# Order of the work ahead of the loop in a three-stage tower kernel: tile 1's tables in buffers of their own, tile 0's b table on GpSimd

## The reference, cut to what matters

```python
# stage 1: 16 channels x 128 heads, 64 complex terms, 1024 positions
Wc = Wc * num * _reciprocal(den * Lam, EPS)
P = dt_Lambda[..., None] * pos - P_max[..., None]
h = jnp.einsum('chn,hnl->chl', Wc, jnp.exp(P)).real
# stage 2: a 1024x1024 weight, masked by blocks of 32x32
h = h + jnp.einsum('bsk,nk->bsn', _layernorm(h), w_masked)
# stage 3: base product, a router of 8 experts with sparsemax, and rank-16 experts
z = _layernorm(h)
h = h + (einsum(z, W_base) + b_base) + sum over experts of weights * (z @ lora_A) @ lora_B
```

## Time and profile before

| | |
|---|---|
| median of 3 runs | 555.26 us (554.86 to 555.58) |
| the profiled execution, time | 552.86 us |
| its span in the trace | 551.0 us |
| its mean granted TensorE clock | 0.978 |

### The profile page before, as it was taken

The page is one execution under the profiler, slowest core; times in us unless marked ns, Lnnn a source line. Parts: engine busy times, 40 slices in busy tenths (PEclk is TensorE's granted clock), DMA queues, the critical chain, the costliest instruction groups (busy, mean ns, idle before and its releaser), DMA issues.

```text
span 551.0 us, 7574 instructions
## 1 busy us (share of the span) xinstructions
PE 498.4 (90%) x2595; PEld 422.0 (77%) x2595; DVE 400.3 (73%) x854; ACT 268.6 (49%) x484; POOL 120.8 (22%) x109
## 2 busy tenths in 40 slices
PE   1446689988999999999999999999999999999995
PEld 0335578766888888888888888888888888888884
DVE  4989987898777777777777869687777677763341
ACT  1655447843918273645546363728191827232200
POOL 0463664713030303020110203030303030303030
PEclk9986879999999999999999999999999999999999
DMA  7991002001010101000010101010101010101011
GB/s 280 399 284 21 0 1 82 7 0 44 1 44 1 43 0 29 14 15 27 7 36 0 43 0 43 0 43 0 43 0 43 2 38 1 38 1 29 11 35 43
DMA packets 17244, 24.06 MB, mean 44 GB/s; under 512 B 9480, under 2 KB 11720, under 8 KB 17224
## 3 DMA queue, kind: packets, MB, share of 16 engines
q1 hardware_dynamic: 16704, 23.54, 14.2%
q10 hardware_dynamic: 520, 0.27, 0.2%
HBM read 15.41 MB, written 8.39 MB: 43 GB/s over the span
## 4 chain that ended last, share of the span: by engine, by line
PE 80%; DVE 13%; issue 2%; ACT 2%; DMA 1%; POOL 0%; ACTq 0%; DVEq 0%; POOLq 0%
PE acc_b L409 34%; PE acc_a L409 28%; PE turnp L386 5%; PE small L433 4%; PE turnp L395 2%; PE turnp L402 2%; PE small L435 1%; DVE mask_sum L970 1%; DVE wa_raw L979 1%; PE acc_b L369 1%; DMA lam_sb<-in_L_tok_Lambda 1%; DVE u_t L1009 1%; DVE wa_lo L986 1%; DVE tmp L1066 1%; DVE gh_t L1008 1%
## 5 line engine op out<-in xcount | busy, mean ns | idle before, releaser
L881 POOL TENSOR_TENSOR h<-h,st 128x1024 f32<-128x1024 f32 x16 | 30.5, 1905 | 349.9 <-PE turnp L402 334.6
L409 PE MATMUL acc_a<-wa_hi,x_hi 128*128 128x512 f32 x256 | 83.7, 403 | 1.9 <-DVE x_lo L1076 1.9
L409 PE MATMUL acc_b<-wb_hi,x_hi 128*128 128x512 f32 x256 | 85.2, 409 | 0.0
L409 PE MATMUL acc_a<-wa_lo,x_hi 128*128 128x512 f32 x256 | 81.0, 392 | 0.0
L409 PE MATMUL acc_a<-wa_hi,x_lo 128*128 128x512 f32 x256 | 80.8, 392 | 0.0
L409 PE MATMUL acc_b<-wb_lo,x_hi 128*128 128x512 f32 x256 | 80.6, 391 | 0.0
L409 PE MATMUL acc_b<-wb_hi,x_lo 128*128 128x512 f32 x256 | 80.5, 391 | 0.0
L617 ACT ACT_TABLE_LOAD x14 | 18.0, 1283 | 101.9 <-DVE b_sb L1068 101.7
L409 PEld LDWEIGHTS acc_a<-wa_hi,x_lo 128*128 128x128 f32 x256 | 48.5, 189 | 10.4
L409 PEld LDWEIGHTS acc_a<-wa_lo,x_hi 128*128 128x128 f32 x256 | 48.5, 190 | 10.1
L409 PEld LDWEIGHTS acc_b<-wb_lo,x_hi 128*128 128x128 f32 x256 | 48.1, 188 | 10.5
(11 more groups left out here) (179 smaller groups left out, 930.9 us busy)
## 6 DMA issues: line engine op xcount, KB each, us to landing
out<-h SPq DMA_DIRECT2D x15, 512.0 KB
mask_raw<-in_L_attn_mask SPq DMA_DIRECT2D x8, 512.0 KB, 10.6
wa_raw<-in_L_attn_weight SPq DMA_DIRECT2D x8, 512.0 KB, 11.2
wb_raw<-in_L_ffn_W_base SPq DMA_DIRECT2D x8, 512.0 KB, 14.8
xn<-in_x SPq DMA_DIRECT2D x15, 64.0 KB
wr_raw<-in_L_ffn_lora_A SPq DMA_DIRECT2D x8, 64.0 KB, 3.3
lb_raw<-in_L_ffn_lora_B SPq DMA_DIRECT2D x1, 512.0 KB, 3.7
bias<-in_L_ffn_b_base SPq DMA_DIRECT2D x1, 512.0 KB, 4.6
```

Source lines behind the costliest of these rows:

```text
L409: return pe.matmul(cols, a, rows, start=first, stop=last)
L881: pool.tensor_tensor(h2[par][:, :], h2[par][:, :], st2[:, par, 1:2].to_broadcast([P, L]), ALU.subtract)\
```

## The change

Seven edits, all ahead of the loop but for three.

1. Tile 1's tables have buffers of their own (`u_1`, `er_1`, `xy_1` and so on, laid over `h2[0]` and over `x1_raw`, the memory of `x1_lo`). `q_arguments(1)` and `phases(1)` stand right behind those of tile 0 on DVE, and `sines(1)` and `q_sines(1)` right behind those of tile 0 on ACT. `exponentials` no longer waits for a b table; `sines` does, from tile 2 on.
2. `table_v` is split: `v_factors` (up to `u12`) is called on its own, earlier, ahead of the loop. For tiles 0 and 1 the second product goes to PSUM (`turnp`), so that the sum reads one operand from PSUM.
3. The b table of tile 0 is made on POOL, right behind `parameters(0)`; `decay_b(0)` is called ahead of it on DVE. Tile 1's stays on DVE, tile 2's on POOL.
4. `BY_POOL` and `CENTRE_LAST` change: POOL makes the low halves of three row blocks (1, 3, 5) in place of four, and centres four (4 to 7) in place of six.
5. `k_low` reads the transposed product in PSUM in place of the copy in `b_sb`; `k_rows` therefore waits for `kt_lo`. This holds in the loop too.
6. In `reciprocal_deviation` the instruction with two tensor operands of one column becomes one with a tensor and two scalar columns. This holds in the loop too, as does the changed wait of edit 1.
7. The constants are issued second on SP's queue in place of first on ACT's; `mask_sums(0)` stands ahead of `signs()`, `dt_transposes()` ahead of `block_sums(0)`; the calls on PE, ACT, POOL and DVE are put in another order up to the loop, among them `phases(2)`, `phases(3)` and `table_v(2)`.

The diff, cut to its core; first buffers, waits and POOL's order, then table_v, k_low, the reciprocal, and the orders of DVE and PE:

```diff
-        BY_POOL = (1, 3, 4, 6)
-        CENTRE_LAST = 2
+        BY_POOL = (1, 3, 5)
+        CENTRE_LAST = 4
...
+        spare, spare_lo = h2[0], x1_raw
+        u_1, er_1 = h_n(spare[:, 0:HT * NM], NM), h_n(spare[:, HT * NM:2 * HT * NM], NM)
...
             sp.dma_start(ldt[:, :], log_dt).then_inc(ldt_in, 16)
+            sp.dma_start(kst[:, :], consts).then_inc(consts_in, 16)
...
             def k_rows(t):
                 pe.wait_ge(kt_hi, t + 1)
+                pe.wait_ge(kt_lo, t + 1)
...
             def exponentials(t):
                 act.wait_ge(tab_exponent, t + 1)
-                if later(t, 1):
-                    act.wait_ge(b_ready, t)
...
             def sines(t):
                 act.wait_ge(tab_phase, t + 1)
+                if later(t, 2):
+                    act.wait_ge(b_ready, 1 if at(t, 2) else t)
...
             def table_b(t):
                 pool.wait_ge(b_chain, t * 3 + 1)
-                pool.wait_ge(h1_ready, t)
-                pool.wait_ge(kt_lo, t)
+                if t > 0:
+                    pool.wait_ge(h1_ready, t)
+                    pool.wait_ge(kt_lo, t)
+                pool.wait_ge(v_chain, t * 4 + 3)
...
             parameters(0)
-            wa_centre(2)
-            wa_centre(3)
+            table_b(0)
+            wa_lows(1)
             wa_centre(4)
-            wa_lows(1)
+            wa_centre(5)
             wa_lows(3)
-            wa_centre(5)
-            wa_lows(4)
             wa_centre(6)
             wa_centre(7)
-            wa_lows(6)
+            wa_lows(5)
             parameters(1)
...
+                second = kt_heads if not later(t, 2) else tmp[:, :].rearrange("p (h a c) -> p h a c", h=HT, a=NA)
...
+                if at(t, 1):
+                    dve.wait_ge(h1_copied, t)
                 dve.wait_ge(v_chain, t * 4 + 3)
                 dve.tensor_tensor(whole(v_sb), w(0), u(0), ALU.mult)
-                dve.tensor_tensor(tmp4, w(1), u(1), ALU.mult).then_inc(v_chain, 1)
+                dve.tensor_tensor(second, w(1), u(1), ALU.mult).then_inc(v_chain, 1)
                 dve.wait_ge(v_chain, t * 4 + 4)
-                dve.tensor_tensor(whole(v_sb), whole(v_sb), tmp4, ALU.add).then_inc(v_ready, 1)
+                dve.tensor_tensor(whole(v_sb), second, whole(v_sb), ALU.add).then_inc(v_ready, 1)
...
-                dve.tensor_tensor(lo[:, :, :], kt_full, hi[:, :, :].bitcast(F), ALU.subtract).then_inc(kt_lo, 1)
+                by_head = lambda v: v[:, :, :].rearrange("p a (h c) -> p h a c", c=C)
+                dve.tensor_tensor(by_head(lo), kt_heads, by_head(hi).bitcast(F), ALU.subtract).then_inc(kt_lo, 1)
...
-                dve.scalar_tensor_tensor(s[:, 6:7], s[:, 5:6], s[:, 5:6], s[:, 4:5], ALU.mult, ALU.mult).then_inc(s_chain, 1)
+                dve.tensor_scalar(s[:, 6:7], s[:, 4:5], s[:, 5:6], s[:, 5:6], ALU.mult, ALU.mult).then_inc(s_chain, 1)
...
             phases(0)
             reciprocal_of_tanh(0)
+            q_arguments(1)
+            phases(1)
+            wa_mask(1)
             mask_sums(2)
-            wa_mask(1)
             mask_sums(3)
             wa_lows(0)
             wa_mask(2)
+            reciprocal_of_norm(0)
+            decay_b(0)
             mask_sums(4)
+            v_factors(0)
             wa_mask(3)
-            reciprocal_of_norm(0)
+            table_v(0)
+            wa_lows(2)
             mask_sums(5)
             wa_mask(4)
-            wa_lows(2)
-            table_v(0)
-            table_b(0)
             mask_sums(6)
-            q_arguments(1)
             wa_mask(5)
-            phases(1)
             mask_sums(7)
             wa_mask(6)
             k_low(0)
             wa_mask(7)
-            wa_lows(5)
+            wa_lows(4)
+            v_factors(1)
             table_v(1)
             table_b(1)
+            wa_lows(6)
             wa_lows(7)
...
             wa_transposes(6)
-            first_attention(0, range(3, 6))
+            first_attention(0, range(2, 4))
             wa_transposes(7)
-            first_attention(0, range(6, KC))
+            first_attention(0, range(4, 6))
...
+            x_transposes(2)
             wb_half(0)
+            wb_half(1)
+            first_attention(0, range(6, KC))
             pe.wait_ge(h1_copied, 1)
             k_transposed(1)
```

More of the change, by code:

```diff
@@ L240, in whole, with phases_of, er_of, sines_of @@
             return b[:, :, :, :]
[L242 to L244 removed]
+        def phases_of(t):
+            return (u_1, k_1, g_1, h_1, a_1) if at(t, 1) else (u_t[:, :, :], k_t, g_t, h_t, a_t[:, :, :])
+        def er_of(t):
+            return er_1 if at(t, 1) else er_t[:, :, :]
+        def sines_of(t):
+            return (xy_1, pp_1, qq_1) if at(t, 1) else (whole(xy), whole(pp), whole(qq))
+        def b_factors(t, i):
+            _, p_, q_ = sines_of(t)
+            return (p_[:, i].unsqueeze(3).to_broadcast([P, HT, NB1, NB0]),
+                    q_[:, i].unsqueeze(2).to_broadcast([P, HT, NB1, NB0]))
         def b_terms(b):
@@ L748, in _ @@
             act.activation(wr[:, :, 0, :], cat_raw, ACT.Copy).then_inc(cat_hi, 1)
-            wb_highs(10)
-            wb_highs(11)
+            wb_highs(4)
+            exponentials(2)
+            wb_highs(5)
+            wb_highs(6)
+            sines(2)
+            wb_highs(7)
+            wb_highs(8)
+            h2_centre(0, 0)
+            wb_highs(9)
+            k_copy(1)
+            for i in range(10, 13):
+                wb_highs(i)
+            h2_high(0)
             k_deviation(1)
-            h2_high(0)
-            wb_highs(12)
             wb_highs(13)
+            wb_highs(14)
             h2_deviation(0, 0)
-            wb_highs(14)
             wb_highs(15)
@@ L1018, in table_v, with v_factors @@
+            def v_factors(t):
                 heads = bass.ds(t * HT, HT)
+                xy_ = sines_of(t)[0]
                 def q(v):
                     return v[:, heads].unsqueeze(1).unsqueeze(3).to_broadcast([P, 2, HT, NA])
+                dve.wait_ge(tab_sin, t + 1)
+                dve.wait_ge(tab_exp, t + 1)
+                if not later(t, 3):
+                    dve.wait_ge(q_ready, 1 if t < 2 else 2)
+                dve.tensor_tensor(xy_, xy_, decay(t, SA, NA), ALU.mult).then_inc(v_chain, 1)
+                dve.wait_ge(v_chain, t * 4 + 1)
+                dve.tensor_tensor(whole(t1), xy_, q(qr), ALU.mult)
+                dve.tensor_tensor(whole(t2), xy_, q(qi), ALU.mult).then_inc(v_chain, 1)
+                dve.wait_ge(v_chain, t * 4 + 2)
+                dve.tensor_tensor(u12[:, 0], t1[:, 0], t2[:, 1], ALU.add)
+                dve.tensor_tensor(u12[:, 1], t1[:, 1], t2[:, 0], ALU.subtract).then_inc(v_chain, 1)
@@ L1023, in w, with table_v @@
+            def table_v(t):
                 def w(r):
@@ L1210, in _ @@
                             small[:, HALF - rt_rows:HALF].rearrange("p (e k) -> p k e", e=E)).then_inc(rt_copied, 1)
+            wb_lows(0)
+            wb_lows(1)
+            h1_reciprocal(0)
+            phases(2)
+            for i in range(2, 5):
+                wb_lows(i)
             k_low(1)
@@ L1219, in _ @@
             wb_lows(9)
-            table_v(2)
-            wb_lows(10)
-            wb_lows(11)
-            decay_b(2)
-            h2_low(0)
-            for i in range(12, 2 * NWT):
-                wb_lows(i)
-            phases(3)
+            decay_b(2)
+            v_factors(2)
+            phases(3)
+            for i in range(10, 13):
+                wb_lows(i)
+            h2_low(0)
+            wb_lows(13)
+            wb_lows(14)
+            wb_lows(15)
+            table_v(2)
             h2_reciprocal(0, 0)
```

178 lines of the change are left out of this document (82 added, 96 removed).

## The result

The changed kernel takes 546.49 us (median of 4 runs, 545.68 to 546.81), the kernel before 555.31 us beside it (554.86 to 555.58): 8.8 us less, ratio 0.984 with a 95% interval of 0.9823 to 0.9857. The profiled execution took 546.28 us, with a span of 544.5 us.

The account below looks back on a forecast made before the run. Prediction: DVE bounds the kernel up to 71 us, PE nearly after. Cumulative gains reach -8.4 us entering the loop; +1.2 for PE's clock gives -7.2, so 555.26 - 7.2 = 548.0 us, range 545.0 to 551.2.

Parts of the forecast that it names:

- The start: Up to `dec`: mask sum and transposes fall into DVE's hole before lambda lands, `dec` at 9.02 instead of 11.44, -2.4 us.
- Tile 0's product: Ahead of the loop on PE: starts at 35.5 instead of 43.0, -7.5 us, with its b table made on POOL.
- First attention product: PE starts attention at 49.0 instead of 55.3, -6.3 us, with `k_low` ending at 44.9.
- The hole: PE's long wait before tile 1's product moves but stays 6.6 us; restart 59.3 instead of 71.2, released by low halves.
- Router and gates: Router product at about 97.8 instead of 103.4, -5.6 us; PE's gates wait shrinks from 2.59 to about 0.4, -7.8 us.
- Edits costed at nothing: `k_low` from PSUM saves nothing, PSUM second product nearest 0, one-column form passes its stall on, counted as empty.
- rival A: DVE/POOL shared port takes it back: stalls return at 17 to 29 us; gain only 4.7, 550.6 us; chance 0.17.
- In the loop: Step stays 29.0 us; `k_rows` waiting for `k_low` has 2.1 us of cover and costs nothing.
- Rival C: Slower: `k_rows` waits for `kt_lo` every step; at 3.1 us late +6.8, 562 us; chance 0.04.
- The clock: PE at half clock behind its hole or at `k_rows`: 2.4 us more or nothing; half taken, +1.2 us.
- the offset of 2.4: Median of runs stands 2.4 us above the profiled execution, so 545.7 profiled became 548.0 us forecast.
- The range: Change in time from -9.5 to about -4 us, from bounds on POOL's b table, PSUM write, clock and start.

Follow-up runs that it names:

- Experiment 8: Changed kernel with the constants issued first on ACT's queue again, ahead of lambda's transfers; 547.75 us.
- Experiment 2: Changed kernel with tile 0's b table back on DVE behind its v table, off POOL; 550.35 us.
- Experiment 10: Changed kernel with the low halves of block 6 on DVE ahead of tile 1's b table, two calls exchanged; 543.53 us.
- Experiment 3: Changed kernel with phases(3) back at its old place behind table_v(2), POOL's b table of tile 2 not waiting for it; 549.55 us.
- experiment 6: Changed kernel with k_low reading the copy in SBUF again and k_rows not waiting for it, all 16 tiles; 548.67 us.
- experiment 5: Changed kernel with the second product of tile 0's v table in SBUF again, tile 1's staying in PSUM; 547.39 us.
- 7: Changed kernel with the one-column instruction in its old form with two tensor operands, in the loop too; 547.50 us.
- Experiment 1: Kernel before with only the change at the start (constants on SP's queue, first activation on ldt, mask sums and transposes earlier); 550.09 us.
- experiment 4: Changed kernel with the second product of tile 1's v table in SBUF, without the wait for h1; 546.17 us.
- 9: Changed kernel with tile 1's arguments and angles moved late into DVE's wait at 39.16, ACT's part behind wa_copies(4); 547.59 us.
- 11: Changed kernel with the last instruction of reciprocal_deviation also given a scalar pointer, so both one-column products have one; 543.75 us.
- 12: Changed kernel with four edits: block 6's low halves earlier, phases(2) in DVE's wait, tile 1's second product in SBUF, both scalar pointers; 539.96 us.

## Why the prediction was right, point by point

The forecast of 548.0 us was 1.5 us above the measured 546.49, inside its range. The chain it follows is the one in the trace, but three terms were mis-sized, and they partly cancel.

- **The start, forecast -2.4, measured -4.3 in the profile.** This term was mis-sized. I let DVE's signs begin where they had, behind lambda's landing at 8.3, and kept the earlier landing for the bounds, by no more than the 0.6 us of its issue. Ahead of the constants on its queue lambda has landed by 3.7. Experiment 8 puts it back: `dec` at 9.29, +1.3 us.
- **Tile 0's product, forecast 35.5, measured 33.46.** Of these 2.0 us 1.9 are the start's; the rest of that sum held: `u12` to product 6.3 us forecast, POOL's table 6.2 measured. Experiment 2 prices the table's place, forecast 3.5, at 3.9 by the medians and 2.3 in its profile, where 2.0 of new stall and 2.4 of a wait that shrank stand against each other.
- **First attention product at 49.0: right by luck, two errors cancelling.** `k_low` ended at 43.8, not at 44.9. But I left out the eight transposes of block 5 ahead of `k_rows`, 1.7 us at half clock, which wait for DVE's low halves (the row at 45.68 above). DVE's wait for block sums was 2.96, forecast "some 2". So of the 1.9 us that the start gave more, nothing was left here.
- **The hole**: forecast 6.6 us, restart 59.3, released by low halves; measured 6.39, 59.35. Experiment 10 shows that two calls in DVE's order make 2.8 us of it, which I had seen and taken as given.
- **Router and gates**: forecast 97.8 and a wait of 0.4; measured 98.0 and 0.19. Experiment 3 prices the move of `phases(3)` at 3.1 us, but not as my sum has it, by PE's wait: without the move PE comes to the gates earlier and waits longer, and it is the clock behind the wait that costs.
- **Edits costed at nothing.** For the change as a whole that was right, since I had charged no stall there. But it hid what they do, counted from `dec` to tile 3's product: `k_low` from PSUM is worth 1.5 us (experiment 6), tile 0's sum from PSUM 1.4 (5), the one-column form 1.2 (7). Each keeps a stall away that a wide instruction of POOL beside it would bring, in experiment 5 the b table, which is new there, in 6 and 7 work that POOL had before; "its operands were free already" looked at waits and not at the port. This is rival A's mechanism, and these edits are a part of why it did not come; all three undone together were not run.
- **In the loop**: step 29.0 in every profile, with and without `k_rows` waiting (experiment 6). Rival C is out.
- **The clock, forecast +1.2, and the offset of 2.4.** The cost was real but elsewhere: in the profile after, the granted clock falls at tile 3's product, as the stretch from 130 to 135 shows. In the profile before it did not fall there. The second and third row go from tile 3's product to the loop, after and before:

```profile
130.00:135.00 5.00, 4.94 (x29) 4.97 (x30) 3.38 (x9) 4.38 (x9) 0.00 (x0) 0.66 0.00 0
...
130.06:149.03 18.97, 18.97 (x98) 16.54 (x98) 12.02 (x31) 12.47 (x23) 0.00 (x0) 0.91 0.01 2
...
138.12:155.57 17.45, 17.45 (x97) 14.84 (x98) 11.85 (x31) 13.54 (x24) 0.00 (x0) 1.00 0.01 2
```

Tile 3's product is 8.1 us earlier and the loop is entered 6.5 earlier (149.03 against 155.57): 1.5 us went there. That this is near the 1.2 of my sum is luck, since I had put it behind the hole and at `k_rows`. For the profiled execution I forecast 545.7, measured 546.28, 0.6 more. The median came out lower by 1.5 us all the same: I had added 2.4 us because the profile before lay under its median, and the changed kernel's lies under its own by 0.2. The upper group of runs before may be falls of the clock. Experiment 1 has the order of the kernel before from tile 0's product on, and its one profile shows two of them. But no run of the upper group was profiled, and the mean granted clocks of the two groups overlap (0.971 to 0.984 in the upper, 0.975 to 0.990 in the lower), so it stays open.

- **The range.** "From -9.5 to about -4" is not what the bounds ahead of it add up to. The low end is -8.4 with nothing for the clock and -0.6 for the start, -9.0. The high ends together, 3.5, 2.4 and 4.8, would undo the gain. The range was a judgement, and that the time lay in it says nothing of those bounds; the start's, -2.4 to -3.0, was left by the measured -4.3.

## What to carry to other kernels

Where two engines share a port, moving work between them pays when the wide work begins after the narrow two-operand work is done, and the engine beside it reads PSUM or scalar pointers: look at each instruction under the moved one, not at the total. A wait removed alone may be given back two places on (experiment 4), and a longer wait may cost nothing itself and much by the clock behind it (experiment 3); look for the pairs of calls in the order that make the large holes. When an input lands at another time in each execution, count a variant's profile from the first instruction that needs it. When a profiled execution lies off its median, don't carry that offset over to the changed kernel.

## What the runs showed of the hardware that I had not expected

Three things. **A 0.45 us earlier issue brought lambda some 4.6 us earlier**: issued at 1.2 and 1.7 us behind the constants it lands at 8.3 to 8.6, issued at 0.7 and 1.3 ahead of them by 3.7. The constants themselves need 2.4 us on that queue, so it is not their end alone that it waits for; whether their place ahead or the mask blocks on the other queue hold it, no run separates. **POOL is held by DVE too** (3.21 in place of 2.35 us, experiment 5). **The clock at a short wait fell in some profiles and not in others**: behind a wait of 2.1 to 2.5 us on PE, tile 3's product took 2.02 us in the profiles before and of experiments 5 and 9, and 2.6 to 3.6 us, with 1.5 to 1.6 us more up to the loop, in the changed kernel and in experiments 1 to 4, 6 to 8 and 10. The kernel before and experiment 1 have the same order and the same wait of 2.42 us there, and it fell in one and not in the other; that one kernel does both is likely from this, but each was profiled once. Behind 1.14 us (11 and 12) it took 2.02 both times. Saving one microsecond of wait there brought the loop 2.5 us nearer.
